# Attention values as the stationary operand on two halves of the array, with row sums added up on GpSimd and VectorE

## The reference

```python
q = split_heads(x @ wq.T) * hd ** -0.25       # 4 heads of 64
k = split_heads(x @ wk.T) * hd ** -0.25
v = split_heads(x @ wv.T)
q, k = _rope(q), _rope(k)
energy = einsum('bhtd,bhld->bhtl', q, k) + causal_mask
out = einsum('bhtl,bhld->bhtd', softmax(energy), v)
x = layernorm(x + out.reshape(B, T, D) @ wo.T)
```

## Time and profile before

| | |
|---|---|
| median of 3 runs | 2279.16 us (2277.18 to 2281.72) |
| the profiled execution | 2283.4 us, of which the span is 2281.6 us |
| mean granted TensorE clock | 0.91 |
| busy share of the span | PE 86%, PEld 77%, DVE 60%, ACT 47%, POOL 45% |
| attention's value matmuls (L486) | first at 84.3 us, last at 1428.4 us |

### The profile page before, as it was taken

One profiled execution on the slowest core, in us unless ns is written; L12 is line 12 of the kernel. 1 busy time (PEld: TensorE's weight loads), 2 busy tenths in 40 slices (PEclk: granted clock), 3 DMA queues, 4 the chain that ended last, 5 costly groups with the idle time before them and its releaser, 6 DMA issues. The chain is left out here.

```text
span 2281.6 us, 40554 instructions
## 1 busy us (share of the span) xinstructions
PE 1953.1 (86%) x13346; PEld 1758.6 (77%) x13346; DVE 1379.7 (60%) x3208; ACT 1071.6 (47%) x2549; POOL 1024.5 (45%) x1683
## 2 busy tenths in 40 slices
PE   4899999999999999999999999352177999999990
PEld 3688888888888888888888878251177999999980
DVE  8444556565566565566565675376794566556645
ACT  3244444444444444444444444124175666666655
POOL 3255444444544454544454211100085667666642
PEclk7799999999999999999999999555588999999995
DMA  2000011111011111011111011220003435554428
GB/s 72 6 19 17 24 38 34 38 43 31 22 38 38 35 39 37 22 38 38 36 38 38 15 43 43 73 99 0 0 1 126 150 135 147 162 167 128 150 51 295
DMA packets 100619, 144.02 MB, mean 63 GB/s; under 512 B 17956, under 2 KB 88592, under 8 KB 96364
## 3 DMA queue, kind: packets, MB, share of 16 engines
q1 hardware_dynamic: 84588, 131.78, 17.1%
q0 software_dynamic: 15872, 10.24, 2.7%
HBM read 112.87 MB, written 39.85 MB: 67 GB/s over the span
## 5 line engine op out<-in xcount | busy, mean ns | idle before, releaser
L582 ACT ACTIVATE probs<-scores_t_ps 128x512 f32<-128x512 f32 (+3 forms) x640 | 341.4, 533 | 649.4 <-PE scores_t_ps L471 355.4
L486 PEld LDWEIGHTS out_ps<-v_sb,probs 128*128 128x128 f32 x4352 | 574.1, 194 | 20.5 <-ACT probs L582 0.4
L486 PE MATMUL out_ps<-v_sb,probs 128*128 128x65 f32 x4352 | 574.4, 272 | 0.0
L683 DVE TENSOR_REDUCE part_max<-scores_ps 128x1 f32<-128x512 f32 (+3 forms) x640 | 383.8, 605 | 160.7 <-PE scores_ps L454 95.3
L833 POOL TENSOR_TENSOR products<-qk,cos_sin 128x128 f32<-128x128 f32 x464 | 199.9, 461 | 337.4 <-ACT qk L559 337.2
L451 PE MATMUL scores_ps<-k_st,q_two 128*128 128x512 f32 (+3 forms) x640 | 275.7, 432 | 21.7 <-DVE q_low L680 12.1
L1443 PE MATMUL up_ps<-xe_t,w 128*128 128x320 f32 x1920 | 289.9, 311 | 1.7 <-DVE xe_t L1550 1.7
L470 PE MATMUL scores_t_ps<-q_two,k_st 128*128 128x512 f32 (+3 forms) x640 | 287.1, 449 | 0.0
L1443 PEld LDWEIGHTS up_ps<-xe_t,w 128*128 128x128 f32 x1920 | 284.6, 189 | 2.3 <-issue 1.9
L471 PE MATMUL scores_t_ps<-q_low,k_one 65*128 65x512 f32 (+3 forms) x640 | 236.3, 369 | 0.0
L1406 POOL DMA_INDIRECT acc_rows<-out_rows,token x96 | 148.7, 1548 | 127.2 <-ACT out_rows L1533 116.2
(11 more groups left out here) (247 smaller groups left out, 3228.1 us busy)
## 6 DMA issues: line engine op xcount, KB each, us to landing
w_raw<-in_w_expert SPq DMA_DIRECT2D x32, 1536.0 KB, 6.5
x_t<-in_x_t SPq DMA_DIRECT2D x128, 128.0 KB, 2.0
w_raw<-in_w_adapter SPq DMA_DIRECT2D x32, 384.0 KB, 7.3
x_row<-in_x SPq DMA_DIRECT2D x64, 128.0 KB, 2.0
x_rows<-x SPq DMA_DIRECT2D x64, 128.0 KB, 2.0
acc_rows<-x SPq DMA_DIRECT2D x64, 128.0 KB, 2.0
ln_x<-acc_rows SPq DMA_DIRECT2D x16, 512.0 KB, 6.3
out_rows_dram<-ln_y SPq DMA_DIRECT2D x16, 512.0 KB, 5.2
```

Of the source, the lines that this page charges most:

```text
L486: mm = pe.matmul(o_ps[:, u % 2, t * OS:t * OS + HD + 1], probs[:, g % P_RING, cols(t)], v_sb[:, kb, h, 0:HD + 1], start=kb == 0 and t == 0 ...
L582: act.activation(probs[:, g % P_RING, i * P:CH], s_ps[:, g % 2, i * P:CH], ACT.Exp).then_inc(exp_done, 1)
L683: dve.tensor_reduce(part_max[:, u % 4, i, c:c + 1], x_ps[:, e % 2, 0:n], AX.X, ALU.max).then_inc(score_read, 1)
```

## The change

The probabilities become the moving operand (up to 512 columns) and the values the stationary one (64 columns). The output is thus transposed: head dimension on the partitions, queries in the columns, and the second head of the pair writes partitions 64 to 127 of the same bank. The chunks of a pair's two heads alternate, and their multiplications are issued in batches of four at every fourth slot. The column of ones is gone; instead GpSimd (even chunks, first head) and VectorE (odd chunks, second head) add the probabilities up in `sums`, and at the end of a group a matmul with ones ("sum") adds over the partitions, in bank "a". "norm" runs once a group on 512 columns. The transposes of "ot" are gone, since the output is transposed already. `probs` has 6 buffers; `x_row` and `hidden` have one in place of two.

```diff
-P_RING = 4
+P_RING = 6
+BATCH = 4
...
-        self.chunks = [(u, kb) for u, n in enumerate(self.size) for kb in range(n)]
+        self.chunks = [(2 * y + hh, kb) for y in range(len(self.groups))
+                       for kb in range(self.size[2 * y]) for hh in range(2)]
...
+        for y, at in enumerate(sum_at):
+            late[at].append(("sum", y))
+            early[at + 1].append(("norm", y))
...
-            late[at].append(("ot", m))
             early[at + 1].append(("ot_read", m))
...
+        def add_up(eng, g):
+            u, kb, i = chunk(g)
+            side = sums[:, u // 2 % 2, u % 2, i * P:CH]
+            eng.wait_ge(exp_done, g + 1)
+            if kb == 0:
+                at_least(eng, totals_ready, u // 2 - 1)
+                eng.tensor_copy(side, probs[:, g % P_RING, i * P:CH]).then_inc(summed[u % 2], 1)
+            else:
+                eng.wait_ge(summed[u % 2], g // 2)
+                eng.tensor_tensor(side, side, probs[:, g % P_RING, i * P:CH], ALU.add).then_inc(summed[u % 2], 1)
...
-            def multiply(g):
+            def multiply(last):
+                for g in range(last - BATCH + 1, last + 1):
...
-                for t in range(i, 4):
-                    mm = pe.matmul(o_ps[:, u % 2, t * OS:t * OS + HD + 1], probs[:, g % P_RING, cols(t)],
-                                   v_sb[:, kb, h, 0:HD + 1], start=kb == 0 and t == 0, stop=kb == 4 * G + t,
+                    mm = pe.matmul(o_ps[hh * HD:(hh + 1) * HD, u // 2 % 2, i * P:CH], v_sb[:, kb, h, :],
+                                   probs[:, g % P_RING, i * P:CH], start=kb == 0, stop=kb == 4 * G + 3,
                                    skip_group_check=True)
...
-                if g < CHUNKS:
+                if g < CHUNKS and g % BATCH == BATCH - 1:
                     multiply(g)
...
-                elif kind == "ot":
...
+                elif kind == "sum":
+                    claim("a", totals_read, k + 1)
+                    for hh in range(2):
+                        pe.wait_ge(summed[hh], begin[k + 1] // 2)
+                        mm = pe.matmul(a_ps[hh * HD:(hh + 1) * HD, :], ones[:], sums[:, k % 2, hh, :],
+                                       start=True, stop=True)
+                    mm.then_inc(totals_ready, 1)
...
-                at_least(act, values_done, g - P_RING + 1)
+                if g >= P_RING:
+                    act.wait_ge(values_done, (g - P_RING) // BATCH + 1)
+                    act.wait_ge(summed[g % 2], (g - P_RING) // 2 + 1)
...
-                    act.copy(attn_t[:, 0].rearrange("p a b -> p (a b)"), b_ps[:, 0:D]).then_inc(attn_upper, 1)
+                    act.copy(attn_t[:, 0], attn[:, :, cols(t)]).then_inc(attn_upper, 1)
...
+                if g < CHUNKS and g % 2 == 1:
+                    add_up(dve, g)
...
-                    dve.reciprocal(norm_by[:, r], out[:, :, HD:HD + 1])
+                    dve.reciprocal(out, a_ps[:]).then_inc(totals_read, 1)
...
+                    dve.wait_ge(values_done, begin[k + 1] // BATCH)
+                    dve.tensor_tensor(out, o_ps[:, r, :], out, ALU.mult).then_inc(attn_ready, 1)
...
-                    dve.tensor_tensor(attn_t[:, 1].rearrange("p a b -> p (a b)"), b_ps[:, 0:D],
+                    dve.tensor_tensor(attn_t[:, 1], attn[:, :, cols(k % NT)], raw(attn_t[:, 0]), ALU.subtract)\
...
+            def main(g):
+                if g < CHUNKS and g % 2 == 0:
+                    add_up(pool, g)
```

More of the change, by code:

```diff
@@ L60 @@
 K_RING = 3
-OS = 66
 def raw(ap):
@@ L78, in __init__ @@
         self.size = [4 * self.groups[y][1] + 4 for y, _ in self.units]
-        self.start = [sum(self.size[:u]) for u in range(len(self.units) + 1)]
-        self.chunks = [(u, kb) for u, n in enumerate(self.size) for kb in range(n)]
+        self.begin = [sum(self.size[:2 * y]) for y in range(len(self.groups) + 1)]
+        self.chunks = [(2 * y + hh, kb) for y in range(len(self.groups))
+                       for kb in range(self.size[2 * y]) for hh in range(2)]
+        begin = self.begin
         total = self.total = len(self.chunks)
         per = total // PH
+        base_of, used = {}, set()
+        for n in range(FIRST, self.PROJ):
+            f, t = divmod(n, NT)
+            base_of[n] = base = 3 * (n - FIRST) if f == 0 else 12 + 4 * t if f == 1 else per * (f - 1) + 5 * t
+            used |= {("a", base), ("a", base + 6)}
+        sum_at = []
+        for y in range(len(self.groups)):
+            at = begin[y + 1]
+            while ("a", at) in used:
+                at += 1
+            used.add(("a", at))
+            sum_at.append(at)
         post, at = [], 0
@@ L86, in __init__ @@
             for t in range(NT):
-                u = 2 * (NG * (2 * b + 1) + t // 4) + 1
-                pace = 8 if self.start[u + 1] < total - per else 5 if self.start[u + 1] < total else 4
-                at = max(at + pace if post else 0, self.start[u + 1] + 1)
+                y = NG * (2 * b + 1) + t // 4
+                pace = 8 if begin[y + 1] < total - per else 5 if begin[y + 1] < total else 4
+                at = max(at + pace if post else 0, sum_at[y] + 1)
                 post.append(at)
@@ L109, in __init__ @@
         for y, (f, G) in enumerate(self.groups):
-            at = self.start[2 * y] - 26
+            at = begin[y] - 2 * self.size[2 * y] - 10
             if y >= Q_RING:
-                at = max(at, self.start[2 * (y - Q_RING + 1)] - 1)
+                at = max(at, begin[y - Q_RING + 1] - 1)
             elif y == 2:
@@ L146, in __init__ @@
             if (c, i) == (self.size[u] // 4 - 1, 3):
-                assert s <= self.start[u] - 3, (u, s, self.start[u])
-                rows.append((min(s + 2, self.start[u] - 3), u))
+                assert s <= begin[y] - 3, (u, s, begin[y])
+                rows.append((min(s + 2, begin[y] - 3), u))
         placed += [(s, u, None, None) for s, u in rows]
@@ L186, in attention @@
     plan = Plan(NB, NT)
-    groups, units, chunks, size, start = plan.groups, plan.units, plan.chunks, plan.size, plan.start
+    groups, units, chunks, size, begin = plan.groups, plan.units, plan.chunks, plan.size, plan.begin
     CHUNKS, COUNT, PROJ = plan.total, plan.COUNT, plan.PROJ
@@ L241, in attention @@
         probs = sb("probs", [P, P_RING, CH])
-        attn = sb("attn", [P, NT, D])
+        sums = sb("sums", [P, 2, 2, CH])
+        ones = sb("ones", [P, HD])
+        attn = sb("attn", [P, 2, NT * P])
         neg_pad = sb("neg_pad", [P, 2, 4, HD + 1])
         part_max = sb("part_max", [P, 4, 4, 4])
-        norm_by = sb("norm_by", [P, 2, 4, 1])
         x_t = sb("x_t", [P, 2, 2, P])
         x_t_parts = sb("x_t_parts", [P, 2, 2, 2, P], F32R)
-        x_row = sb("x_row", [P, 2, D])
+        x_row = sb("x_row", [P, D])
         w_qkv = sb("w_qkv", [P, 2, 2, 3 * D], F32R)
@@ L279, in attention @@
         xt_loaded = [sem(f"xt_loaded{r}") for r in range(2)]
-        xrow_loaded = [sem(f"xrow_loaded{r}") for r in range(2)]
+        xrow_loaded = sem("xrow_loaded")
         xt_upper, xt_split, v_copied = sem("xt_upper"), sem("xt_split"), sem("v_copied")
@@ L351, in _ @@
                 load_xt(n)
-            for m in range(2):
-                load_row(m)
+            load_row(0)
             def step(kind, k):
@@ L510, in step @@
                     turn_heads(q_bank(k), q_rows[:, k % ROW_RING]).then_inc(qt_turned, 1)
-                elif kind == "ot":
[L512 to L516, removed]
-                    mm.then_inc(attn_turned, 1)
+                elif kind == "sum":
[5 more added lines that the diff above has]
+                    mm.then_inc(totals_ready, 1)
                 elif kind == "wo":
                     claim("b", resid_done, k + 1)
+                    pe.wait_ge(attn_split, k + 1)
                     if k == 0:
```

85 lines of the change are left out of this document (40 added, 45 removed).

## The result

The changed kernel takes **2720.24 us** (median of 4 runs, 2717.94 to 2721.2) against 2278.86 (4 runs), a ratio of **1.193, interval 1.191 to 1.196**: slower by 441 us, where 2221 was forecast and 2390 was the upper edge. The value matmuls start from 93.1 to 1857.5 us, before from 84.3 to 1428.4, so the attention stage itself has grown from 1345 to 1765 us; what follows its last start is about as long as before (859 and 853 us).

The account below looks back on a forecast made before the run. The prediction took TensorE to bound the attention stage: 2283.4 us of the profiled execution, less 108 on TensorE, plus 50 given back, made 2225, and 2221 for the median, 4 us lower. The range was 2150 to 2390.

Parts of the forecast that it names:

- What bounds the kernel: Attention stage: TensorE, busy 1251.9 of 1300 us, sets the pace, so a microsecond taken from it is worth one.
- Removed and added on TensorE: Attention matmuls: 467 us removed, 336 added with overlapping halves, 23 for changes of tile shape, together -108 us.
- five steps of a batch: Value matmuls: the eight instructions of a batch, on two overlapping halves, take five steps of time instead of eight.
- matmuls start in order: TensorE's queue: claimed that matmuls start in order, so eight instructions take five steps and a sum's four take three.
- The serial rival: Value matmuls: the two halves stream one after the other, TensorE gains 83 us, total 2387 us; chance 0.30.
- The loads: Value matmuls: loads of the new stationary operand hide under moving columns and cost nothing; otherwise 65 us worse.
- Norm, 17 us more: VectorE's norm: two operations of 512 columns a group at 0.685 us, 44 us for the old product's 27.
- Turns of VectorE and GpSimd, 101 us: Attention stage: VectorE meets a busy GpSimd in 74% of 416 cases, waiting 0.33 us each, 101 us.
- Half given back, 50 us: Attention stage: of VectorE's 101 us of waits, half, 50 us, comes back as lost time, between 0 and 101.
- Waits at no cost: Attention stage: waits of the exponential, the sum and the single x_row buffer cost nothing; GpSimd's queue was called doubtful.
- The third: Attention stage: halves overlap but GpSimd and VectorE set the pace, 101 and 69 us lost, 2341 us; chance 0.17.
- The last test of the prediction: Attention stage: forecast wrong if TensorE's busy share falls under 85% without the stage getting shorter.

Follow-up runs that it names:

- b1: The kernel before the change with 1664 of its 4352 value matmuls taken out and nothing added: 2173.03 us.
- e4: The changed kernel with a batch's four chunks issued first head, first head, second head, second head instead of alternating: 2725.41 us.
- e17: e7 with a fourth buffer of turned queries, which evens out the row-max scores, and first-chunk copies one column wide: 2275.62 us.
- e5: The changed kernel with each whole batch of value matmuls writing one half of the partitions, the next batch the other: 2840.45 us.
- e7: e6 with the reciprocal replaced by a copy and every row-sum add cut to one column: 2353.80 us.
- e16: e6 with all row-sum adds on VectorE: 2565.35 us.
- e6: The changed kernel with queries turned 50 slots ahead and at most two row-max scores put into a slot, nothing left out: 2601.97 us.
- e11: e6 with every row-sum add cut to one column, the reciprocal of 512 columns kept: 2460.52 us.
- e8: e6 with sums landing with queries on partitions, a reciprocal of 128 x 8, and an identity matmul spreading the result: 2582.49 us.
- e15: e6 with all row-sum adds on GpSimd: 2638.22 us.

## Why the prediction was wrong, step by step

- **What bounds the kernel.** "A microsecond taken from it is worth one as long as no other engine comes near the length of the stage": this step failed. It read 96% busy as the whole story. In b1 the other engines' work is unchanged, far from the length of the stage, and a microsecond is worth 0.4 (111 of the estimated 280). By that measure the -108 of TensorE would not have shown in full even without new work elsewhere.
- **Removed and added on TensorE** (-108). Right in kind, a little too careful: five steps of a batch were forecast, 2.17 us, and 1.87 to the next start was measured, four steps of 0.433 plus 0.14 for loads and changes of shape. What failed in it is "matmuls start in order": by that e4's order would have taken 3.0 us a batch, and it took 1.87. e17's busy time is 122 lower. The serial rival (0.30) was wrong, as the batch of 1.87 us and e5 show. The loads stay hidden for the most part. The Trainium skill's rule ("TensorE: Matmul & The Clock Gate", packing small matmuls) that a load overlaps only where the row group differs would have made a batch longer by up to 8 x 0.046 = 0.37 us, an estimate, over and above the shape change, and there are 0.14 for both; the same section lets a load to the background weight buffer go ahead too, and that would agree.
- **Norm, 17 us more.** Failed: "the reduction's price; the reciprocal of so many columns is not in the trace". The trace showed a reciprocal of four columns alone (0.169 us), and a term that no row shows at its size should have had its upper end from there, which scales to far more than 0.685. With 3.36 us its term is 32 x (3.36 + 0.69) - 27 = 103 us of VectorE instead of 17, and by e7 it is worth 107 of the time.
- **Turns of VectorE and GpSimd, 101 us.** The mechanism was right, the total near by some luck. VectorE's adds take 238.6 us where 288 at e16's 0.657 make 189; the split of `attn_t` (L719 before, L752 after) takes 33.8 against 25.3; together 58, where adds and split were forecast at 86. The third operation in the forecast (L752 before, L784 after) is not longer at all (23.7 us against 24.7), and the layernorm product, which reads one SBUF tensor and was not in the forecast, takes 56.4 against 25.0, which brings the sum to 89. Nor is a wait "about half an operation": the longest add on VectorE takes 3.77 us. GpSimd's adds were mis-sized: 1.26 us for 512 columns (median in e6) against 1.08.
- **Half given back, 50 us.** Failed: mis-sized. The slack was taken as one sum over the stage, and the full time of the turns as the most that could come back. The sums alone cost 128 to 141 us. From e11 to e6, where only the width of the adds differs, TensorE's idle time in the stage rises from 241 to 330 us and its busy time from 1265 to 1319, at a granted clock of 0.88 instead of 0.91.
- **Waits at no cost, and the plan.** The largest omission: the plan's new order of row-max scores stands in the sum at nothing, and the diff's lines on when queries are turned were not worked through. 22 slots with 8 to 19 scores cost 118 us (e6), and with what e17 evens out up to 196.
- **The rivals.** The third ("GpSimd and VectorE set the pace", 2341) named the right side and the right waits, `x` L859 among them with 55 us; its price lacked the reciprocal and the plan. The last test of the prediction ("falls under 85% without the stage getting shorter") is what came: 80%.

## What to carry to other kernels

An engine that is 96% busy can still cover others' in-order stretches: before pricing what is taken from it, ask which waits its work hides, since in b1 six tenths came back as idle time and lower clock. Where a plan places work by slots, work out the distribution of the changed plan, not only the durations of its instructions. An operation that no row shows at its size gets a wide bound from the smaller one, and adds over SBUF were cheapest here on VectorE alone (2565 us), dearer shared with GpSimd (2602) and dearest on GpSimd alone (2638).

## What the runs showed of the hardware that was not expected

- VectorE's reciprocal costs by its columns: 3.36 us for 512 and 0.207 for 8 (e8), 6.3 ns a column between them, where a copy of 512 columns takes 0.69 (e7).
- Two float32 matmuls on the two halves of the array's columns stream at the same time (eight take 1.87 us to the next start, 3.57 in one half), in either order of issue.
- An operation of VectorE with a single SBUF tensor and two scalars is held up by GpSimd's adds too: the layernorm product takes 0.436 us when GpSimd has no adds (e16), 0.836 to 1.145 when it has half of them (e6, e8) and 1.313 when it has all (e15).
